# Alternating PSUM bank pairs, four slot weight products in a row, and es transposes ahead of the second q/k tile in a fused attention and MLP layer

## The reference

```python
xn = layernorm(x)
q, k = rope(xn @ Wq.T), rope(xn @ Wk.T)      # 16 heads of 128
v, g = xn @ Wv.T, xn @ Wg.T
s = clip(xn @ Ws1.T @ Ws2.T + bs2, -32, 32)  # 64 slots a head
es, enz = exp(s), exp(-cumlogsumexp(s, time))
A  = where(causal, q @ k.T * scale, 0)
ok = enz * (A @ es)                          # per token and slot
qv = softmax(ok, slots)
W2 = where(causal, (qv * enz) @ es.T, 0)     # the slot weights
o  = rmsnorm(W2 @ v) * g_norm * silu(g)
attn = o @ Wo.T
# MLP of width 2048; gate, up and down weights are 4-bit codes with block scales
ffn = (gelu(xn @ Wgate.T) * (xn @ Wup.T)) @ Wdown.T
out = x + attn + ffn
```

## Time and profile before

| what | value |
|---|---|
| time, median of three runs | 1156.21 us (1155.81 to 1157.9) |
| the profiled execution's own time | 1157.08 us |
| its span, first to last instruction | 1155.4 us |
| mean granted TensorE clock | 0.988 |
| TensorE matmuls busy (PE) | 1109.4 us, 96% |
| VectorE busy (DVE) | 949.0 us, 82% |
| ScalarE busy (ACT) | 640.4 us, 55% |
| GpSimd busy (POOL) | 421.8 us, 37% |
| DMA | 23.03 MB, mean 20 GB/s |
| chain that ended last | PE 81%, DVE 5%, issue 4%, ACT 2%, POOL 1% |

### The profile page before, as it was taken

How to read it: one execution, slowest core, us unless ns; L and a number is a source line. 1 busy time by engine, 2 the same in 40 slices (tenths; PEclk the granted TensorE clock), 3 DMA queues, 4 the chain that set the end, 5 groups by cost and what they waited for, 6 DMA issues and landing times.

```text
span 1155.4 us, 19869 instructions
## 1 busy us (share of the span) xinstructions
PE 1109.4 (96%) x6872; PEld 936.8 (81%) x6872; DVE 949.0 (82%) x1808; ACT 640.4 (55%) x1748; POOL 421.8 (37%) x306
## 2 busy tenths in 40 slices
PE   5779999999999999999999999999999999999995
PEld 4558888888888888888888888888888888888875
DVE  5978888788888888888887888888888888888772
ACT  4455466555645656554655556464574556655551
POOL 4323244432424335232453324343252334523230
PEclk9899999999999999999999999999999999999997
DMA  4002000020002000020000200001000200000001
GB/s 161 1 1 75 2 1 2 1 76 1 2 1 76 1 1 2 1 76 1 1 1 1 75 1 1 2 35 41 1 1 2 75 2 1 2 1 20 12 10 35
DMA packets 9109, 23.03 MB, mean 20 GB/s; under 512 B 817, under 2 KB 5809, under 8 KB 7985
## 3 DMA queue, kind: packets, MB, share of 16 engines
q1 hardware_dynamic: 9008, 21.76, 5.1%
HBM read 19.66 MB, written 2.10 MB: 19 GB/s over the span
## 4 chain that ended last, share of the span: by engine, by line
PE 81%; DVE 5%; issue 4%; ACT 2%; POOL 1%; POOLq 0%; DVEq 0%; ACTq 0%
PE bank L194 19%; PE bank L196 18%; PE bank L195 18%; PE bank L283 4%; PE bank L315 3%; PE bank L340 3%; PE bank L296 3%; PE bank L285 2%; PE bank L329 2%; PE bank L332 2%; PE bank L331 2%; DVE og L757 1%; PE bank L299 1%; PE bank L307 1%; PE bank L273 1%
## 5 line engine op out<-in xcount | busy, mean ns | idle before, releaser
L1083 POOL TENSOR_TENSOR inter_lo<-ffb,inter_hi 128x512 fp32r<-128x512 f32 x64 | 83.5, 1331 | 417.5 <-ACT inter_hi L605 417.5
L1074 POOL TENSOR_TENSOR qkT<-ra,xs 128x512 f32<-128x512 f32 x128 | 164.2, 1283 | 109.4 <-DVE xs L848 77.2
L574 ACT ACTIVATE sm<-bank,mx 128x64 f32<-128x64 f32 x256 | 76.5, 325 | 154.3 <-DVE mx L804 154.3
L845 DVE TENSOR_TENSOR ra<-bank,rope 128x512 f32<-128x512 f32 x128 | 87.7, 685 | 48.3 <-ACT xs L556 47.2
L793 DVE RECIPROCAL enzT<-enzT 128x256 f32<-128x256 f32 x64 | 111.5, 1743 | 0.0
L848 DVE TENSOR_TENSOR xs<-xs,rope 128x512 f32<-128x512 f32 x128 | 110.9, 866 | 0.0
L194 PE MATMUL bank<-xh,wqk_hi 128*128 128x512 f32 x256 | 110.3, 431 | 0.0
L194 PE MATMUL bank<-xh,wgu_hi 128*128 128x512 f32 x256 | 106.4, 416 | 0.0
L579 ACT ACTIVATE At<-bank 128x128 f32<-128x128 f32 x128 | 35.4, 276 | 126.6 <-DVE At L728 126.6
L196 PE MATMUL bank<-xh,wqk_lo 128*128 128x512 f32 x256 | 101.7, 397 | 0.0
L196 PE MATMUL bank<-xh,wgu_lo 128*128 128x512 f32 x256 | 101.5, 397 | 0.0
(11 more groups left out here) (137 smaller groups left out, 3187.1 us busy)
## 6 DMA issues: line engine op xcount, KB each, us to landing
raw<-in_w_qkvg SPq DMA_DIRECT2D x8, 1024.0 KB, 5.0
scaled<-in_w_scaled SPq DMA_DIRECT2D x8, 640.0 KB, 7.5
packed<-in_w_packed SPq DMA_DIRECT2D x8, 384.0 KB, 5.5
acc<-in_x SPq DMA_DIRECT2D x4, 512.0 KB, 7.7
out<-acc SPq DMA_DIRECT2D x4, 512.0 KB, 2.9
ws_raw<-in_w_slot SPq DMA_DIRECT2D x8, 48.0 KB, 1.7
rope<-in_rope_tab SPq DMA_DIRECT2D x1, 256.0 KB, 5.8
osq<-in_w_slot SPq DMA_DIRECT2D x1, 128.0 KB, 3.9
```

Source lines behind the costliest of these rows:

```text
L574: ins = act.activation(sm[:, c], src[:, c], ACT.Exp, bias=mx[:, g:g + 1], accum_out=ssum[:, g:g + 1])
L845: dve.tensor_tensor(two(ra[i % 2][:, :]), two(pj[i][:, :]), cos, ALU.mult).then_inc(cos_done, 1)
L1074: pool.tensor_tensor(qkT[:, i, :], ra[i % 2][:, :], xs[i % 2][:, :], ALU.add).then_inc(roped, 1)
L1083: pool.tensor_tensor(inter[1][e][:, :], ffb[e][:, :], inter[0][e][:, :].bitcast(F32), ALU.subtract).then_inc(inter_lo, 1)
```

## The change

Three things are done, in stages 1 to 30 (stage 0 keeps its interleaving, and the last stage has no next one to project for):

1. The bank pairs swap roles. `own(st)` is the pair that has slot reads, outputs, softmax and es transposes; `other(st)` has scores, slot scores and the L307 transposes. From stage 1 on the roles alternate. Slot weight products 0 and 1 go to `other(st)`, 2 and 3 to `own(st)`; values go to `own(st + 1)`, which is `other(st)`.
2. The es transposes move from behind q/k tile 1 to ahead of it, with the wait for `acc_done` (VectorE's add of the second output share, L819, which frees the bank) in front of them. `copy_J` moves ahead of swap 1 on ScalarE.
3. All four slot weight products stand in a row; q/k tile 2 moves behind them. In front of products 2 and 3 the wait for `W_off` is replaced by one for `J_ready` (the copy of the es transposes). VectorE and ScalarE read all four in a row. cos and sin of tile 1 move behind VectorE's four diagonals; ScalarE's `split_hi` of the gate/up weights (at `bp` 3) and swap 2 move behind its four copies.

The core of the diff:

```diff
+        def own(st):
+            return rg if st == 0 or st % 2 else sc
+        def other(st):
+            return sc if st == 0 or st % 2 else rg
+        def score_bank(st, i):
+            return other(st)[i % 2]
+        def weight_bank(st, i):
+            return (other(st) if i < 2 or st == 0 else own(st))[i % 2]
...
@@ TensorE, stage
                 if not last:
                     project_qk(st + 1, nbp, nhp, 0)
+                if not first:
+                    pe.wait_ge(acc_done, 2 * st)
+                if not last:
+                    pe.wait_ge(es_ready, st + 2)
+                    slot_transpose(own(st)[0], esT[nbp % 2])
                     project_qk(st + 1, nbp, nhp, 1)
                 pe.wait_ge(qe_ready, st + 1)
                 if not last:
-                    pe.wait_ge(es_ready, st + 2)
-                    slot_transpose(rg[1], esT[nbp % 2])
                     pe.wait_ge(clip_done, st + 2)
                 slot_weights(st, bp, 0)
-                if not last:
+                if first:
                     project_qk(st + 1, nbp, nhp, 2)
-                if first:
                     transpose_x(3)
-                pe.wait_ge(W_off, 4 * st + 2)
+                    pe.wait_ge(W_off, 4 * st + 2)
+                elif not last:
+                    pe.wait_ge(J_ready, st + 2)
                 slot_weights(st, bp, 1)
                 if not last:
+                    if not first:
+                        project_qk(st + 1, nbp, nhp, 2)
                     project_qk(st + 1, nbp, nhp, 3)
                 pe.wait_ge(v_ready, 4 * st + 4)
                 if first:
                     slot_inner(3, rg[1])
-                else:
-                    pe.wait_ge(acc_done, 2 * st)
                 values(st, bp, 0)
                 if first:
                     pe.wait_ge(h1_done, 8)
                     pe.wait_ge(h1_lo, 4)
-                elif not last:
-                    pe.wait_ge(J_ready, st + 2)
                 values(st, bp, 1)
@@ ScalarE, stage
                 if not last:
                     swap_halves(st + 1, 0)
+                    copy_J(st + 1, own(st)[0][:, :])
                     swap_halves(st + 1, 1)
-                    copy_J(st + 1, rg[1][:, :])
                 off_diagonal(*w_args, 0, 1.0)
                 off_diagonal(*w_args, 1, 1.0)
+                if first:
+                    swap_halves(st + 1, 2)
+                    x_hi(3)
+                off_diagonal(*w_args, 2, 1.0)
+                off_diagonal(*w_args, 3, 1.0)
                 if bp == 3 and more:
                     split_hi(hp + 1, W_GU)
                 if bp == 2 and more:
                     split_slot(hp + 1)
                 if not last:
-                    swap_halves(st + 1, 2)
-                if first:
-                    x_hi(3)
-                off_diagonal(*w_args, 2, 1.0)
-                off_diagonal(*w_args, 3, 1.0)
-                if not last:
+                    if not first:
+                        swap_halves(st + 1, 2)
                     swap_halves(st + 1, 3)
@@ VectorE, stage
                 diagonal(*w_args, 0, mask_w, (o_full, 2 * st))
                 diagonal(*w_args, 1, mask_w, (o_full, 2 * st))
-                if not last:
+                if first:
                     rope_cos(st + 1, 1)
                     rope_sin(st + 1, 1)
-                if first:
                     x_lo(3)
                 diagonal(*w_args, 2, mask_w, (o_full, 2 * st))
                 diagonal(*w_args, 3, mask_w, (o_full, 2 * st))
                 if not last:
-                    rope_cos(st + 1, 2)
-                    rope_sin(st + 1, 2)
-                    rope_cos(st + 1, 3)
-                    rope_sin(st + 1, 3)
+                    for i in range(2 if first else 1, 4):
+                        rope_cos(st + 1, i)
+                        rope_sin(st + 1, i)
```

More of the change, by code:

```diff
@@ L267, in slot_scores @@
                     pe.wait_ge(ws2_lo, 4 * hp + 4)
-                pe.matmul(sc[0][:, :] if n is not None else sc[1][:, :],
+                pe.matmul(other(n)[0][:, :] if n is not None else sc[1][:, :],
                           ws2[:, :], h1[:, bp, :], start=True, stop=True).then_inc(S_full, 1)
@@ L293, in slot_reads @@
                     c = b * T
-                    halves = [(rg[0][h * M:(h + 1) * M, :], At[2 * h + b], slice(h * M, (h + 1) * M)) for h in range(2)]
+                    halves = [(own(st)[0][h * M:(h + 1) * M, :], At[2 * h + b], slice(h * M, (h + 1) * M)) for h in range(2)]
                     for dst, a, m in halves:
@@ L304, in slot_rows @@
                 pe.wait_ge(okz_done, st + 1)
-                dst = sc[1]
+                dst = other(st)[1]
                 for i in range(NT):
@@ L312, in slot_weights @@
                 t0 = b * T
-                pair = [(sc[h], slice(h * M, (h + 1) * M)) for h in range(2)]
+                pair = [(weight_bank(st, 2 * b + h), slice(h * M, (h + 1) * M)) for h in range(2)]
                 for dst, g in pair:
@@ L356, in outputs @@
                         src = ogT if s < 2 else inter
-                        mm = three(pe, rg[1 - b][:, tt * D:(tt + 1) * D],
+                        mm = three(pe, own(done)[1 - b][:, tt * D:(tt + 1) * D],
                                    [src[u][s % 2][:, cols] for u in range(2)],
@@ L570, in softmax_exp @@
                 wait(act, rs_done, st)
-                src = sc[1]
+                src = other(st)[1]
                 for g in range(8):
@@ L757, in gate_o @@
                     ins = dve.scalar_tensor_tensor(
-                        out=og[:, c], in0=rg[b][:, q * P:(q + 1) * P], scalar=scal[:, 4 * b + q:4 * b + q + 1],
+                        out=og[:, c], in0=own(done)[b][:, q * P:(q + 1) * P], scalar=scal[:, 4 * b + q:4 * b + q + 1],
                         in1=G[par][:, c], op0=ALU.mult, op1=ALU.mult)
@@ L965, in stage @@
                 if not last:
-                    clip(st + 1, npar, sc[0][:, :])
+                    clip(st + 1, npar, other(st)[0][:, :])
                 if not first:
```

56 lines of the change are left out of this document (28 added, 28 removed).

## The result

| | before | after |
|---|---|---|
| median of the runs made side by side | 1157.48 us (1155.81 to 1157.91) | 1161.36 us (1160.05 to 1162.54) |
| ratio, 95% interval | | 1.0037 (1.0028 to 1.0046) |
| span of the profiled execution | 1155.4 us | 1158.8 us |

What follows compares the result with a forecast made beforehand. VectorE's and GpSimd's chain to the gating was taken to set three stage ends in four, despite TensorE 96% busy. Terms 2.1 + 4.7 - 2.1 - 0.8 - 1.3 = +2.6 us gave a median of 1158.8, range 1155.2 to 1162.5.

Steps and rivals of the forecast that it cites:

- bp 0 to 1: Seven stage ends: gating 0.15 us later, TensorE 0.4 earlier, so they just meet; -0.3 us each.
- TensorE's saving of 0.4 a stage: From q/k tile 0 to the values, TensorE's steps take 7.78 us instead of 8.17.
- No new wait on TensorE: Es transposes and third product find their inputs ready, with 0.7 and 0.6 us of cover; no cost.
- bp 1 to 2 and 2 to 3: Fourteen stage ends: later rotate 1, swap 3 and a stretched sin 3 delay the chain; +0.15 us each.
- bp 3 to 0: Seven stage ends: GpSimd's gate/up weight part starts later and holds sin 2 and rotate 2; +0.67 us each.
- The wait of L340: TensorE's wait for gating at the gated transposes: about 0.8 us in bp 2 and 3, 1.8 in bp 0.
- Stages 30 and 31: Two stages without decoding ahead of them, with a microsecond of room: -0.4 us each.
- Last stage: Second product pair follows at once, but values fall more into a slowed granted clock: -1.3 us, between -0.9 and -2.4.
- the 1.58 of the working: In the last stage, values start 1.58 us earlier, at 1128.08 instead of 1129.66.
- TensorE's saving reaches the end: Rival: tile 3, not rotate 1, releases swap 3, drawing the chain forward; 13.3 us saved, 1142.9 us; chance 0.10.

Runs made afterwards that it cites:

- e6: Early es transposes and new banks kept; q/k tile 2 back between the product pairs, VectorE and ScalarE orders as before: 1155.39 us, ratio 0.9985 against the kernel before.
- e5: The changed kernel with the es transposes behind q/k tile 1 again and the es copy behind swap 1: 1185.8 us, ratio 1.0255 against the kernel before.
- e2: The changed kernel with VectorE's and ScalarE's orders both as before, TensorE's four products still in a row: 1156.02 us, ratio 0.9987 against the kernel before.
- e3: The changed kernel with only ScalarE's gate/up weight split back ahead of its copies 2 and 3: 1159.24 us, ratio 1.002 against the kernel before.
- f1: The changed kernel with VectorE's five decode steps moved from the stages' ends to the middle: 1155.3 us, ratio 0.9988 against the kernel before.
- f2: f1 plus an earlier gate/up weight split on ScalarE and GpSimd, off the rotates: 1148.63 us, ratio 0.9928 against the kernel before.
- e4: New alternating bank roles kept, every engine's order of work as in the kernel before: 1155.52 us, ratio 0.9982 against the kernel before.
- f6: f3 with decode step 4 moved behind the inversion: 1149.51 us, ratio 0.993 against the kernel before.
- f3: The kernel before with the decode and weight-split moves of f2: 1154.37 us, ratio 0.9978 against the kernel before.
- f5: f2 with decode step 4 behind the inversion and, at bp 3, ScalarE's second hidden-layer part behind the es copy: 1139.16 us, ratio 0.9843 against the kernel before.

## Why the prediction was right, point by point

The forecast, slower with 1158.8 in a range of 1155.2 to 1162.5, holds: 1161.36, or +3.4 us by the spans for a sum of +2.6. The main mechanism was right: TensorE's saving is spent at the gated transposes, and the late weight part on GpSimd is the largest loss. That the sum came out so near is in part luck, since two terms were off in opposite directions, bp 0 to 1 and the last stage.

- **TensorE's saving of 0.4 a stage**: 7.77 for 8.17, with four products in 1.50 where I took 1.51. The joined products and the early transposes have the steps that the trace of before said. By e6 the whole saving hangs on the joined products; the transposes' shorter step is paid back by tiles 0 and 1, as in the working.
- **No new wait on TensorE**: right; the es copy ended 0.66 ahead of the third product (I had 0.6), and e5 shows the price of that cover gone, 0.8 us a stage.
- **bp 1 to 2 and 2 to 3, +0.15 each**: 0.20 in the columns bp 2 and bp 3, 14 times, so 2.8 for 2.1. The last link was the one named: sin 3 held until 0.55 behind rotate 2, which I put at 561.1 and which ended at 561.16 on that clock. The working had both paths to it, the late rotate 1 with swap 3 and the late swap 2 with rotate 2, but it charged the 0.15 to the diagonals' place. e2 shows that TensorE's tile 2 behind all products is enough for it. The size was nearly right, its cause was named wrongly.
- **bp 3 to 0, +0.67 each**: 0.71, 7 times, 5.0 for 4.7. The weight part started 0.69 later. e2 takes it back, e3 shows that ScalarE's split isn't its cause, and from f1 to f2, where the weight part leaves its place between the rotates, the stage falls from 35.16 to 33.69.
  The wait of L340 that I gave, 1.8 us, is not there: by the weight loads' idle time it is 1.18 in stage 16 and 1.02 in stage 14, for 0.92 and 0.40 before.
- **bp 0 to 1, -0.3**: -0.22, 7 times, so -1.5 for -2.1. TensorE and the chain just meet there, as said; the weight loads of L352 wait 0.38 us.
- **Stages 30 and 31, -0.4 each**: -0.41 in stage 30. The second was named wrongly: stage 31 has no next stage's tiles in it and so nothing to save there, and belongs to the end. The other -0.41 is stage 1, which the sum had left out.
- **Last stage, -1.3, between -0.9 and -2.4**: about -2.0, and of this about 1.6 is the granted clock. The pairs follow each other at once, and the values wait only for the copies. Rows of after, then one of its stretches of 3 us:

```profile
1132.06 0.70 PE L327 MATMUL bank<-qe,esT 64*128 64x256 f32 x4 [1.07 <-DVE qe L855]
...
1132.79 0.63 PE L327 MATMUL bank<-qe,esT 64*128 64x256 f32 x4
...
1134.23 0.46 PE L341 MATMUL bank<-vS,Wt 128*128 128x128 f32 x2 [0.59 <-ACT Wt L593]
```

```profile
1134.00:1137.00 3.00, 2.77 (x24) 2.75 (x24) 0.96 (x3) 1.24 (x4) 0.00 (x0) 1.00 0.02 5
```

  From the first product to the values it takes 1134.23 - 1132.06 = 2.17 us; before it was 1129.66 - 1125.99 = 3.67, so 1.5 less for the 1.58 of the working. But the values did not fall into half clock as the working had it. The granted clock (third number from the end) is 1.00 while they run, and from their start to that of the gated transposes it takes 1143.14 - 1134.23 = 8.91 for 1139.45 - 1129.66 = 9.79 before, where they began in the stretch of the earlier trace rows; of the 1.17 us for which TensorE stood idle in front of the second pair, 0.59 is left, in front of the values. Some 0.7 is lost again ahead of them, where TensorE waits 1.66 us behind the gated transposes for VectorE's `ogT_lo` (L780), in place of 1.06 before and 1.07 in e4; why that comes later is not shown.
  How much of this is the change? f6 answers it: in its last stage it has the instructions and the order of before, and the granted clock stayed at 1.00 while the products and the values ran.

```profile
1121.74 0.70 PE L315 MATMUL bank<-qe,esT 64*128 64x256 f32 x4 [1.17 <-ACT Wt L579]
...
1122.59 0.49 PE L329 MATMUL bank<-vS,Wt 128*128 128x128 f32 x2
...
1131.53 1.97 PE L340 MATMUL bank<-ident,og 128*128 128x128 f32 x8 [6.00 <-DVE og L758]
```

  The second pair takes 1122.59 - 1121.74 = 0.85 us to the values, for 1129.66 - 1128.08 = 1.58 before, and from the values to the gated transposes it is 1131.53 - 1122.59 = 8.94, for 9.79. So the stage takes 35.49 there, for 37.07 before and 38.33 in f3, all three with the same work in it; against f6 the changed last stage saves 0.1 us. The 1.58 of the working had held 0.73 of half clock without saying so.

The sum is 0.8 short of the spans' difference: the 14 stages (0.7), bp 3 to 0 (0.3) and bp 0 to 1 (0.6) came out dearer, the end 0.7 cheaper. That is +0.9, and 0.8 without the roundings. With a last stage like f6's in the kernel before, the spans would lie about 5 us apart and not 3.4 (an estimate, 3.4 + 1.6).

Of the rivals, "TensorE's saving reaches the end" did not come, and its condition was not met: rotate 1 ended later than tile 3. But the condition would not have been enough. In e2 rotate 1 ends at 558.54 + 1.30 = 559.84, just ahead of the values' start behind tile 3 (559.85), and those stages still take 34.13: ScalarE is at its copies until swap 3, and sin 3 meets rotate 2. The saving gets through in all kinds of stages only in f5, where the decoding and the weight part are off the chain. What the rival priced at 13.3 us came to 10.35 there.

## What to carry to other kernels

Here TensorE was 96% busy, and a saving on it was still lost, because another engine's chain set the point where they meet: read which wait ends last in each kind of stage before counting a saving, and take the distance from there. Moving one engine's instructions forward means asking what now stands behind them on each of the others; here two diagonals of 0.67 us pushed a long GpSimd instruction, and that pushed the whole chain. And a change that loses may be half of one that wins: run it again with the chain shortened before it is given up. Last, compare stretches that the change touches with the same stretches before, and look at the granted clock in them: here the last stage gave back 2.0 us, and 1.6 of it was the clock.
